# Feed-forward normalisation by folded weights and a late scale, on one core

## The reference, cut to what matters

```
x = inputs                                  # 4 x 2048 tokens x 256
x = x + attention_a(layernorm(x))           # linear attention, 16 heads
x = x + ffn(layernorm(x))
x = x + attention_b(layernorm(x))           # acts on the first 16 tokens of each batch; all others get only + ob
x = x + ffn(layernorm(x))

layernorm(x) = (x - mean(x)) / sqrt(var(x) + 1e-5)
ffn(z) = relu(z @ Ws1)**2 @ Ws2 + routed    # Ws1 256 x 128, Ws2 128 x 256
routed = sum over experts of trunc(prob) * relu(z @ W1[e])**2 @ W2[e]
```

## Time and profile before

| | |
|---|---|
| median of 3 runs | 490.48 us (489.87 to 493.17) |
| the profiled execution, its own time | 493.28 us |
| its span | 491.4 us |
| PE busy | 452.9 us, 92% |
| DVE, ACT, POOL busy | 307.2, 249.2, 175.1 us |
| mean granted clock of PE | 0.965 of full |
| share of the chain that ended last | PE 69%, DVE 13%, POOL 5%, ACT 5% |

### The profile page before, as it was taken

The page is one execution under the profiler, slowest core; times in us unless marked ns, Lnnn a source line. Parts: engine busy times, 40 slices in busy tenths (PEclk is TensorE's granted clock), DMA queues, the critical chain, the costliest instruction groups (busy, mean ns, idle before and its releaser), DMA issues.

```text
span 491.4 us, 8138 instructions
## 1 busy us (share of the span) xinstructions
PE 452.9 (92%) x2695; PEld 368.9 (75%) x2695; DVE 307.2 (63%) x788; ACT 249.2 (51%) x415; POOL 175.1 (36%) x253
## 2 busy tenths in 40 slices
PE   7699989999999998779999999999999999996763
PEld 4589979889998887568787787687778786884441
DVE  5445674565544535365767867787877977695462
ACT  3345545545455432436575546565665574756330
POOL 2334533333543500332435425454341644224300
PEclk9979999999999999789999999999999999999995
DMA  8411211111100011000112011011101110111110
GB/s 275 132 45 46 84 44 43 45 43 43 43 0 1 0 39 51 1 1 1 61 30 68 2 45 44 2 45 45 44 3 44 45 45 1 45 44 45 45 43 7
DMA packets 22659, 20.74 MB, mean 42 GB/s; under 512 B 2950, under 2 KB 22604, under 8 KB 22604
## 3 DMA queue, kind: packets, MB, share of 16 engines
q1 hardware_dynamic: 22044, 19.53, 12.5%
q10 hardware_dynamic: 560, 0.52, 0.3%
HBM read 11.53 MB, written 8.45 MB: 41 GB/s over the span
## 4 chain that ended last, share of the span: by engine, by line
PE 69%; DVE 13%; POOL 5%; ACT 5%; issue 4%; DMA 2%; SPq 2%; POOLq 0%; DVEq 0%; ACTq 0%
PE PG L1152 11%; PE PA L1237 8%; PE PG L1242 5%; PE PA L1256 4%; PE PT L1229 4%; PE PB L1242 3%; DVE ln_bn L667 3%; ACT scratch L509 3%; PE PA L1142 3%; PE PA L1143 3%; PE PA L1144 3%; PE PB L1129 3%; PE PB L1130 3%; PE PB L1128 3%; PE PT L1084 2%
## 5 line engine op out<-in xcount | busy, mean ns | idle before, releaser
L509 ACT ACTIVATE scratch<-x_all,ln_shift,ln_rstd 128x256 f32<-128x256 f32 (+2 forms) x188 | 97.4, 589 | 79.3 <-POOL ln_shift L433 44.6
L427 POOL TENSOR_SCALAR ln_rstd<-ln_mv 128x4 f32<-128x4 f32 x48 | 10.8, 226 | 220.6 <-DVE ln_mv L670 207.3
L667 DVE BATCH_NORM_STATS2 ln_bn<-x_all 128x6 f32<-128x256 f32 (+1 forms) x188 | 65.8, 412 | 0.6
L1237 PE MATMUL PA<-scratch,ws 128*128 128x512 f32 x128 | 61.5, 604 | 1.5 <-ACT scratch L612 1.2
L1152 PE MATMUL PG<-scratch 128*128 128x256 f32 x256 | 60.8, 392 | 1.3 <-DVE scratch L747 1.3
L747 DVE SCALAR_TENSOR_TENSOR scratch<-scratch,PB 128x1024 f32<-128x1024 f32 x16 | 19.6, 1223 | 65.0 <-ACT scratch L544 65.0
L1152 PEld LDWEIGHTS PG<-scratch 128*128 128x128 f32 x256 | 49.4, 198 | 8.2 <-issue 1.5
L440 POOL TENSOR_TENSOR x_all<-x_all,ob_rows 128x1024 f32<-128x1024 f32 x16 | 37.8, 2362 | 41.9 <-ACT scratch L509 41.9
L429 POOL TENSOR_TENSOR ln_rstd<-ln_rstd,minus_half 128x4 f32<-128x4 f32 x48 | 49.8, 1038 | 4.0
L1229 PE MATMUL PT<-ident,scratch 128*128 128x128 f32 x256 | 36.8, 290 | 9.9 <-ACT scratch L509 9.2
L1229 PEld LDWEIGHTS PT<-ident,scratch 128*128 128x128 f32 x256 | 29.9, 149 | 15.4 <-ACT scratch L509 11.6
(11 more groups left out here) (213 smaller groups left out, 938.4 us busy)
## 6 DMA issues: line engine op xcount, KB each, us to landing
out_dram<-scratch SPq DMA_DIRECT2D x16, 512.0 KB, 2.9
x_all<-n_L_attn_a_inputs_q_dram SPq DMA_DIRECT2D x15, 512.0 KB, 3.6
x_all<-n_L_attn_a_inputs_q_dram ACTq DMA_DIRECT2D x2, 128.0 KB, 3.1
x_all<-n_L_attn_a_inputs_q_dram SPq DMA_DIRECT2D x2, 128.0 KB, 2.9
scratch<-in_L_attn_a_Wk_dram SPq DMA_DIRECT2D x1, 256.0 KB, 5.0
scratch<-in_L_attn_a_Wq_dram ACTq DMA_DIRECT2D x1, 256.0 KB, 5.2
scratch<-in_L_attn_a_Wv_dram SPq DMA_DIRECT2D x1, 256.0 KB, 6.5
scratch<-in_L_attn_a_Wo_dram SPq DMA_DIRECT2D x1, 256.0 KB, 6.1
```

What stands on the lines that cost most here:

```text
L509: nc.scalar.activation(dst[:, t:t + 1, 0:width], x_tile(n, t)[:, :, 0:width], ACT.Identity, scale=ln_rstd[:, slot, t:t + 1], bias=ln_shift ...
L667: nc.vector.bn_stats(ln_bn[:, slot, t:t + 1, :], x_tile(n, t)).then_inc(bn, 1)
L1237: last = mm(dst, ws1[:, c, :], xt[:, c, :], start=(c == 0), stop=(c == C - 1))
```

## The change

Both feed-forwards share their weights. With c = centred ws1 (`w1c`, each column less its mean), relu(layernorm(x) @ ws1) is relu(x @ c) divided by the deviation, so the square carries 1/variance as a factor. The kernel now transposes x itself, not a normalised copy:

- At step 0 PE, ACT and DVE make `w1c`, `wc` = ws2 @ w1c, and the bias term (`fold_ffn`, `fold_ffn_product`).
- Group i-1: PE transposes x (now first in the step, into PA), `hidden` with `w1c` into PT, relu and square on ACT. POOL makes 1/(4 var) (`rsq`), PE spreads it over the partitions by four transposes, DVE multiplies (`h2s`), `down` to PB. The second feed-forward's inner sum is the same PSUM plus one product `wc` with `h2s`; so the second normalisation, its eight transposes, its copy and its `hidden` are gone. ACT makes relu and square `h3` at the end of the step.
- Group i-2: `down` of `h3` to PA; the output is x plus this sum times 1/(4 var) of the second statistics: tiles 0 and 1 by DVE, tiles 2 and 3 scaled by ACT and added by POOL, in place in `x_all`. The pipeline is three groups deep.
- The division of o, the transposes of o and w use PB and PA; the chain has PG alone, `attention_b_has_read` is gone. On DVE, place "y" of the chain now stands ahead of the addition of w.
- SP gathers each batch's 16 tokens in the step in which they are ready (`gather`).
- POOL makes the scale of group 1 before it waits for `w2_loaded`.

```diff
@@ SP
+            def gather(r):
+                sp.wait_ge(o_mm, 2)
+                sp.wait_ge(f2_added, r + 1)
+                sp.dma_start(xs[r * SPT:(r + 1) * SPT, :], x_all[0:SPT, r * G * T, :]).then_inc(c_xs, 16)
+
             def step(g, b):
...
+                r = lagged(g, b, 1)[0]
+                if runs(r):
+                    load_experts(2 * r)
+                    if r < B:
+                        gather(r)
+                    load_experts(2 * r + 1)
@@ POOL
             ln1(0)
             pool.wait_ge(norm1_dve, 2)
+            ln1(1)
             pool.wait_ge(w2_loaded, 16 * 8)
-            with pool.Fori(1, NG) as n:
+            add_bo(0)
+            with pool.Fori(2, NG) as n:
...
+            def rsq(slot, j, bn, powed, done):
+                a, d, both = ln_a[:, slot, :], ln_d[:, slot, :], ln_bn[:, slot, :, :]
+                pool.wait_ge(bn, T * (j + 1))
+                nc.gpsimd.tensor_tensor(a, both[:, :, 2], both[:, :, 5], ALU.add).then_inc(powed, 1)
+                nc.gpsimd.tensor_tensor(d, both[:, :, 1], both[:, :, 4], ALU.subtract).then_inc(powed, 1)
...
+                nc.gpsimd.tensor_tensor(ln_rsq[:, slot, :], a, minus_ones[:, :], ALU.pow).then_inc(done, 1)
@@ ACT
-                    normalise(y3, nu, 1, u, rstd3, norm3)
-                    nc.scalar.activation(x3t, PT[:, :, :], ACT.Copy).then_inc(t3_done, 1)
-                    normalise(y2, lagged(g, b, 0)[1], 0, i, rstd2, norm2)
+                    for t in range(2, T):
+                        nc.scalar.activation(y3[:, t - 2:t - 1, :], four(PA)[:, t:t + 1, :], ACT.Copy,
+                                             scale=ln_rsq[:, 1, t:t + 1]).then_inc(f4_scaled, 1)
@@ DVE
                 if runs(v):
                     dve.wait_ge(f4_mm, v + 1)
-                    nc.vector.tensor_tensor(x_out, four(PB), x_group(nv), ALU.add).then_inc(f4_added, 1)
+                    dve.wait_ge(rsq3, v + 1)
+                    for t in range(2):
+                        nc.vector.scalar_tensor_tensor(x_tile(nv, t), four(PA)[:, t:t + 1, :], ln_rsq[:, 1, t:t + 1], x_tile(nv, t),
+                                                       ALU.mult, ALU.add).then_inc(out_dve, 1)
...
+                    nc.vector.tensor_tensor(h2s, h2, PT[:, 1, :], ALU.mult).then_inc(f1_scaled, 1)
+                attention_b(g, b, "y")
                 if runs(i):
                     dve.wait_ge(w_mm, i + 1)
-                    nc.vector.tensor_tensor(x_group(n), four(PB), x_group(n), ALU.add).then_inc(w_added, 1)
+                    nc.vector.tensor_tensor(x_group(n), four(PA), x_group(n), ALU.add).then_inc(w_added, 1)
...
-                attention_b(g, b, "y")
@@ PE
+                if runs(r):
+                    pe.wait_ge(w_added, r + 1)
+                    for c in range(C):
+                        for t in range(T):
+                            last = nc.tensor.transpose(PA[:, c, t * P:(t + 1) * P], x_all[:, nr * T + t, c * P:(c + 1) * P], ident[:, :])
...
                 if runs(r):
-                    hidden(PA[:, 0, :], x2t, f1_mm, t2_done, C * r, 1)
+                    pe.wait_ge(rsq2, r + 1)
+                    for t in range(T):
+                        last = nc.tensor.transpose(PT[:, 1, t * P:(t + 1) * P], ln_rsq[:, 0, t:t + 1].to_broadcast([P, P]), ident[:, :])
+                    last.then_inc(r2_mm, 1)
...
-                    transposes(PT, y3, t3_mm)
...
+                    pe.wait_ge(f1_scaled, r + 1)
+                    mm(PT[:, 0, :], wc, h2s, start=False, stop=True, skip_group_check=True).then_inc(f3_mm, 1)
+                    down(PB, h2s, f2_mm)
```

More of the change, by code:

```diff
@@ L471, in chain_rstd @@
+                if runs(r):
+                    run_experts(r)
             def chain_rstd(k):
@@ new lines, in run_experts @@
+            def run_experts(r, n, i):
+                with pe.If(routed > 0):
+                    pe.wait_ge(f2_added, r + 1)
+                    pe.wait_ge(w_added, min(i + 1, NG))
+                    for k in (2 * r, 2 * r + 1):
+                        if k % 2:
+                            for c in range(C):
+                                for t in range(T):
+                                    last = nc.tensor.transpose(PA[:, c, t * P:(t + 1) * P], x_all[:, n * T + t, c * P:(c + 1) * P], ident[:, :])
+                                last.then_inc(r_t3, 1)
+                            pe.wait_ge(r_t3_sb, C * (r + 1))
+                            for c in range(C):
+                                mm(PT[:, 0, :], w1c[:, c, :], x2t[:, c, :], start=(c == 0), stop=(c == C - 1))
+                        for c in range(C):
+                            last = mm(PA[:, 1, :], ones_f[:, :], x2t[:, c, :], start=(c == 0), stop=(c == C - 1))
+                        last.then_inc(r_sums, 1)
+                        pe.wait_ge(r_turned, 6 * k + 3)
+                        for c in range(C):
+                            last = mm(PA[:, 1, :], ones_f[:, :], squares[:, c, :], start=(c == 0), stop=(c == C - 1))
+                        last.then_inc(r_sums, 1)
+                        pe.wait_ge(r_turned, 6 * k + 6)
+                        experts(k, P, T, x2t, four(PB), h2)
@@ L1263, in step @@
                     pe.wait_ge(f3_sq, v + 1)
-                    ge(pe, w_added, min(i, NG) if isinstance(i, int) else i)
-                    down(PB, h3, f4_mm)
-                    run_experts(routed_ordinal(g, b, 0), P, T, x3t, four(PB), h3,
-                                [(f4_added, v + 1), (t3_done, v + 1)] + ([(o_done, 3 * (i + 1))] if runs(i) else []))
+                    pe.wait_ge(t2_done, min(C * (r + 1), C * NG))
+                    down(PA, h3, f4_mm)
+                attention_b(g, b, "x")
@@ L1268, in step @@
                 if runs(r):
-                    pe.wait_ge(norm2, T * (r + 1))
-                    ge(pe, t3_done, i - 2)
-                    if runs(i):
-                        pe.wait_ge(o_done, 3 * i + 1)
-                    transposes(PT, y2, t2_mm)
+                    if r == 0:
+                        pe.wait_ge(fold_sb, 4)
+                    ge(pe, f3_relu, r)
+                    for c in range(C):
+                        pe.wait_ge(t2_done, C * r + c + 1)
+                        last = mm(PT[:, 0, :], w1c[:, c, :], x2t[:, c, :], start=(c == 0), stop=(c == C - 1))
@@ L1375, in attention_b @@
                     return
-                if place == "before x":
-                    return
-                if place == "x":
-                    wait(f3_relu, min(i - 2, NG) if isinstance(i, int) else i - 2)
-                else:
-                    wait(f2_added, min(i, NG) if isinstance(i, int) else i)
                 if it is None:
```

521 lines of the change are left out of this document (285 added, 236 removed).

## The result

The changed kernel takes 514.94 us (median of 4 runs, 513.38 to 515.62), the kernel before 491.4 in the same runs: a ratio of 1.0499 [1.045, 1.0548], 5% slower. I had forecast 492.0, with 481 to 503 as the range. The forecast is wrong, and the miss of 22.9 us is the thing to explain. The profiled execution has a span of 511.6 us and a time of its own of 513.38.

The account below looks back on a forecast made before the run. PE's own work was taken as the bound in steps 8 to 15. Terms -4.8 - 5.2 + 9.4 + 1.4 + 0.3 + 0.4 gave +1.5 us on 493.28, so 494.8, or 492 on the median; range 481 to 503.

Parts of the forecast that it names:

- The net 1.56 us less of PE work in a step: Every step: transposes and a hidden product go, fewer are added; a step without chain work is 13.4 us of PE.
- the 0.57 of waiting at o_hi: Every step: PE waits about 0.57 us for o_hi, formerly covered by hidden; bounds zero to 1.0, plain step 14.1 us.
- Step 4 is the largest term: Step 4: the chain's 34 transfers start behind a gather, DVE and PE wait; 24.35 us against 14.94, 9.4 more.
- Pass 1: Start: POOL begins 1.9 us earlier and group 1's products avoid half clock; 4.8 us less, bounds 1.9 and 5.
- steps 5 to 7: Less PE work, but a half-clock start and waits for chain work on DVE; 53.6 us, 1.4 more.
- steps 8 to 15: 118.7 us of PE work plus waits at o_hi and for DVE's chain work; 131.5 us, 0.3 more.
- place "y", priced at 7.2: Steps 8 to 15: chain work ahead of DVE's additions makes them late, 7.2 us in all.
- the start at half clock: Step 5: after standing still for 10 us PE starts at its lower clock level, 2.8 us added.
- Through the same links: Drain: one feed-forward less, but DVE waits behind POOL's longer queue; 48.2 us against 47.81, 0.4 more.
- steps 0 to 3: Folding added in step 0, steps 0 and 1 end at 27.1 us; 55.3 against 60.45, 5.2 less.
- The rivals: Transfers not late, 479, chance 0.12; DVE and ACT late by half, 484, 0.15; PE's clock falls at waits, 504, 0.18.
- Rival 3: PE's clock falls at waits after two chain places; four falls, about 3 us each, make 504; chance 0.18.

Follow-up runs that it names:

- the second execution: The kernel before, unchanged, profiled once more to check its first profiled execution: 486.8 us.
- the first correction's run: Changed kernel, with POOL's two large additions in steps 5, 7, 8, 12 and 16 waiting for the chain's normalisation on DVE: 498.54 us, ratio 1.0184.

## Why the prediction was wrong, by its own steps

**Right.** The net 1.56 us less of PE work in a step, and the 0.57 of waiting at o_hi: steps 2 and 3 are 13.82 us for the 14.1 worked out. Steps 0 and 1: 26.8 for 27.1. The transfers: all of "Step 4 is the largest term" is confirmed by the changed kernel's rows (12.11 and 10.10 us of wait, as forecast) and by their removal (10.27 us). Pass 1 ended at 179.98 for 180.0.

**Right in the sum, in part by luck.** Once the collision is out, steps 5 to 7 and 8 to 15 are 53.96 and 131.14 us for 53.6 and 131.5, but their terms are not those of the forecast. In steps 8 to 15 PE is busy for 123.99 us where I had 118.7, so 7.1 less than before and not 12.5, though a step without chain work (13.46 for 14.89) does show 1.43 of the 1.56; why the steps with chain work save less, no run shows. And PE's waits are 7.15 us and not 12.8: place "y", priced at 7.2, costs 3.8, four waits of up to 1.0 for `f2_added`, and none for `w_added`. In steps 5 to 7 the sum has a slip: 2.8, three times 0.57, twice 0.9 and 3.4 make 9.7, not 8.8, and the start at half clock was 1.6, not 2.8.

**Wrong, the step that failed:** durations of DVE's instructions, taken as fixed. Every DVE instruction of the chain was priced at what it took in the kernel before, in "Steps 5 to 7", "Steps 8 to 15" and "Drain", and I moved POOL's instructions without asking what runs beside them. "Place y after b = 0 waits for POOL and then does two products of 0.67" leaves out the two products L1084 and L1085 ahead of these, 0.83 us before and 3.93 now. Taking the collision out gave 15.2 us by stretch: 8.0 in steps 5 to 7, 6.7 in 8 to 15, 0.5 in the drain (16.4 by the medians, 15.4 by the ratios).

**Wrong, the drain.** "Through the same links" assumed that the chain waits for its own operand. It waited in DVE's queue behind an output tile of another group, for POOL's 1/variance. Moving it ahead of that tile gave 5.6 us, and the drain is then 46.22 us, 2.0 under my 48.2; which term that is, no run shows. In the order of the queues both `rsq3` ahead of L939 and the chain's copy behind it were to be seen.

**The remainder, and the reference point.** The misses by stretch are 18.6 us of the 22.9. The other 4.4 are my own step from the profiled execution to the median: I took off the 2.8 us by which the kernel before stood above its median there, while the changed kernel's stood 1.6 below. That execution of before was no fair reference for the gains either: 2.6 of the 4.8 us of pass 1 (184.77 against 182.19) and 3.6 of the 5.2 of steps 0 to 3 (6.2 earlier at step 3, less the 2.6) are missing in the second one. What differs between the two executions are the landing of the first transfers, 1.5 us later in the first, and 13.6 us more at half clock; how much each costs was not taken apart. So the forecast lengths of these stretches were right, and over half of what they seemed to gain, 6.2 of 10.0, was none; against the second execution, span 484.9, the changed kernel is 26.7 us behind.

**The rivals.** None of them happened, and none was this. Rival 3 named the clock's fall at PE's waits: it did fall, at waits of 2 to 3.8 us that came from the collision, three times at 1.7 us or less, not four times at 3. The length of a wait alone does not tell these rows apart. Over steps 8 to 15 of the first correction's run, with waits of 0.36 to 1.0 us, the granted clock stayed at 1.00, and so it did behind the 3.05 us ahead of step 13 of the changed kernel; but in step 10 with place y last a wait of 1.15 to 1.17 us for o_lo was followed by 3.4 us at half clock, in two different kernels, and one of 1.33 in step 14 was not. The Trainium skill ("TensorE: Matmul & The Clock Gate", section "A second HAM failure mode: psum-queue depth-cycling") has the clock swing with frequent brief idle stretches between groups of products. By that, steps 8 to 15 of the first correction's run would have swung, and they did not; step 10 of the other two did.

## What to carry to other kernels

Before an instruction of POOL is moved, list what DVE runs beside it at the new place, and price DVE's instructions with two SBUF operands, and its copies and scalings within SBUF, as the sum of both. In a new trace compare durations by line with the old ones before reading any wait: a wait elsewhere may only be an instruction that has grown. Where a wait is put ahead of a queue, list what stands behind it in the drain too; and take the reference for a sum from more than one execution, its clock row beside it.

## What the runs showed of the hardware

- DVE and POOL stop each other on reads of SBUF. DVE's 64x256 product of two SBUF operands: 0.42 us alone or beside POOL's memset, 2.56 behind POOL's addition of 2.35, 1.37 behind one of 1.44. The Trainium skill ("SBUF — State Buffer", section "Who interferes with whom") says that a VectorE instruction with two SBUF inputs contends with a GpSimd instruction that reads SBUF and not with one that only writes, and the traces agree on both halves. That whoever issues first keeps the shared ports for the whole instruction it says of VectorE's two-port modes; these products waited for POOL's additions to their end as well, but not for POOL's one-operand multiplication, 1.5 us before whose end DVE came through.
- It goes the other way round as well. In step 10 of the changed kernel DVE was first by 0.16 us, and POOL's addition, 1.26 us otherwise, took 2.27; in step 11 a copy of DVE within SBUF, 0.28 us in the kernel before, took 1.28 behind POOL:

```profile
365.01 1.28 DVE L1105 TENSOR_TENSOR q_all<-q_all,b_weights 64x1024 f32<-64x1024 f32 x1
365.17 2.27 POOL L502 TENSOR_TENSOR x_all<-x_all,scratch 128x512 f32<-128x512 f32 x1
...
380.70 1.26 POOL L502 TENSOR_TENSOR x_all<-x_all,scratch 128x512 f32<-128x512 f32 x1
380.83 1.28 DVE L1111 COPY q_all<-b_weights 64x256 f32<-64x256 f32 x1
```

- DVE's instructions with one operand in PSUM are not touched: the additions of PSUM to x_all (L961 and L969 of the changed kernel) take 1.15 to 1.23 us, and 1.21 and 1.23 beside POOL's additions in the first experiment's run (at 326.61 and 459.90), and the two tiles of L939 0.87 us, with POOL's L440 started 0.14 us before them (362.85 and 362.99).
